# GpSimd's three-part splits and bias additions as two instructions each

## The reference

```
x = layernorm(x + self_attention(x))        # 16 heads of 16, ALiBi bias on the keys
x = layernorm(x + cross_attention(x, ctx))  # ctx: 16 x 120 x 256, padded keys masked by -1e9
x = layernorm(x + moe(x))                   # 8 experts, 256 -> 1024 -> 256, relu, top 2 by softmax

qh, kh, vh = x @ Wq + bq, kv @ Wk + bk, kv @ Wv + bv
scores     = qh . kh / 4 + bias;   attn = softmax(scores);   out = (attn @ vh) @ Wo + bo
```

## Time and profile before

| | |
|---|---|
| median of 3 runs | 1312.58 us (1311.31 to 1317.23) |
| the profiled execution's own time | 1317.72 us |
| its span, first to last instruction | 1315.8 us |
| busy in the span: PE, DVE | 1088.9 us (83%), 976.3 us (74%) |
| busy in the span: ACT, POOL | 567.6 us (43%), 489.3 us (37%) |
| granted TensorE clock over the span | 0.933 of full speed |

### The profile page before, as it was taken

One profiled execution on the slowest core, in us unless ns is written; L12 is line 12 of the kernel. 1 busy time (PEld: TensorE's weight loads), 2 busy tenths in 40 slices (PEclk: granted clock), 3 DMA queues, 4 the chain that ended last, 5 costly groups with the idle time before them and its releaser, 6 DMA issues. The chain is left out here.

```text
span 1315.8 us, 32466 instructions
## 1 busy us (share of the span) xinstructions
PE 1088.9 (83%) x9894; PEld 773.2 (59%) x9895; DVE 976.3 (74%) x2213; ACT 567.6 (43%) x1025; POOL 489.3 (37%) x603
## 2 busy tenths in 40 slices
PE   3778989999888889989998661889999999999970
PEld 2445666666665566656665441667777777777750
DVE  1568888888887888888887663577777777777754
ACT  1434555555554566666665420223222323232325
POOL 1233343334433435545552574022322322322224
PEclk7889999999999899999998865899999999999995
DMA  8577866686648488879886676652222222222228
GB/s 179 136 179 162 193 141 180 175 206 135 164 96 188 114 234 240 196 218 262 240 207 196 205 244 234 247 166 45 40 44 43 43 43 42 42 44 40 45 30 259
DMA packets 153666, 193.98 MB, mean 147 GB/s; under 512 B 30636, under 2 KB 133948, under 8 KB 149323
## 3 DMA queue, kind: packets, MB, share of 16 engines
q1 hardware_dynamic: 139144, 174.67, 49.8%
q0 software_dynamic: 13296, 17.83, 8.1%
q10 hardware_dynamic: 1152, 0.53, 0.2%
HBM read 122.63 MB, written 66.16 MB: 143 GB/s over the span
## 5 line engine op out<-in xcount | busy, mean ns | idle before, releaser
L1397 PE MATMUL HB<-xhi,W 128*128 128x128 f16 x2272 | 292.0, 221 | 21.6 <-issue 16.6
L1397 PEld LDWEIGHTS HB<-xhi,W 128*128 x2272 | 202.0, 98 | 66.1 <-issue 48.1
L1602 POOL DMA_INDIRECT d_sums<-ysc,tok x71 | 111.0, 1563 | 322.3 <-ACT ysc L1463 208.5
L1397 PE MATMUL HB<-xlo,W 128*128 128x128 f16 x1136 | 225.0, 220 | 0.0
L836 DVE TENSOR_REDUCE peaks<-SA 128x4 f32<-128x1024 f32 x128 | 156.6, 1223 | 65.9 <-PE SA L688 65.4
L1113 ACT ACTIVATE PT<-SB 128x1024 f32<-128x1024 f32 x128 | 131.1, 1024 | 130.9 <-PE SB L736 128.9
L1397 PEld LDWEIGHTS HB<-xlo,W 128*128 x1136 | 111.9, 98 | 49.7
L1519 DVE SCALAR_TENSOR_TENSOR hlo<-HB,hhi 128x512 f16<-128x512 f32 x142 | 98.2, 692 | 55.4 <-ACT hhi L1455 51.6
L1455 ACT ACTIVATE hhi<-HB 128x512 f16<-128x512 f32 x142 | 84.2, 593 | 119.7 <-DVE HB L1511 119.5
L1463 ACT ACTIVATE ysc<-yb,wv 128x256 f32<-128x256 f32 x71 | 36.1, 508 | 192.0 <-DVE yb L1543 183.9
L1511 DVE SCALAR_TENSOR_TENSOR HB<-HB,SC,b1c 128x512 f32<-128x512 f32 x142 | 107.1, 754 | 13.9 <-PE HB L1397 7.9
(11 more groups left out here) (205 smaller groups left out, 2375.0 us busy)
## 6 DMA issues: line engine op xcount, KB each, us to landing
wst<-in_w SPq DMA_DIRECT2D x32, 1024.0 KB, 10.1
d_w<-w SPq DMA_DIRECT2D x16, 1024.0 KB, 8.2
W<-d_w SPq DMA_DIRECT2D x16, 1024.0 KB, 7.2
k_stack<-d_k SPq DMA_DIRECT2D x96, 128.0 KB
XB<-d_rows SPq DMA_DIRECT2D x65, 130.0 KB
d_q<-q_part SPq DMA_DIRECT2D x16, 384.0 KB, 6.0
d_k<-k_part SPq DMA_DIRECT2D x16, 384.0 KB, 2.7
q_stack<-d_q SPq DMA_DIRECT2D x16, 384.0 KB, 4.5
```

Of the source, the lines that this page charges most:

```text
L1397: mm = pe.matmul(out, w.rearrange("p e n -> p (e n)"), x[n % 2][:, k, :], start=(k == 0 and half == 0 and x is xhi), stop=(k == KT - 1 and ...
L1602: pool.indirect_dma_start(YS, bass.IndirectOffsetOnAxis(ap=tok[n % 6][:, 0:1], axis=0), ysc[n % 2][:, :], None, compute_op=ALU.add).then_i ...
```

## The change

A split is done in six instructions rather than three, each of the three operations once for feature half 0 and once for half 1. The wait between operations comes behind both halves, so the two halves of one operation stand back to back, with no wait between. `x1bo` and `xbo` are done in two instructions each, one for each of the two token tiles (QT = 2); the semaphore rises with the second. The arithmetic, the tensors and the DMAs are the same. 221 GpSimd instructions are added (63 x 3 + 32).

```
--- before.py
+++ after.py
@@ -1185,11 +1185,16 @@
             if not on(b):
                 return
             wait(pool, f"part0_{n}", b + 1)
-            chain(pool.tensor_tensor(rest[n][:, :, :], full[n][:, :, :], part[n][:, :, 0, :], ALU.subtract))
-            chain(pool.tensor_tensor(part[n][:, :, 1, :], rest[n][:, :, :],
-                                     minus[:, 2:3].unsqueeze(1).to_broadcast([P, KT, width[n]]), ALU.add))
-            pool.tensor_tensor(part[n][:, :, 2, :], rest[n][:, :, :], part[n][:, :, 1, :], ALU.subtract
-                               ).then_inc(sem(f"parts_{n}"), 1)
+            for k in range(KT):
+                chain.put(pool.tensor_tensor(rest[n][:, k, :], full[n][:, k, :], part[n][:, k, 0, :], ALU.subtract))
+            chain.wait()
+            for k in range(KT):
+                chain.put(pool.tensor_tensor(part[n][:, k, 1, :], rest[n][:, k, :],
+                                             minus[:, 2:3].to_broadcast([P, width[n]]), ALU.add))
+            chain.wait()
+            for k in range(KT):
+                ins = pool.tensor_tensor(part[n][:, k, 2, :], rest[n][:, k, :], part[n][:, k, 1, :], ALU.subtract)
+            ins.then_inc(sem(f"parts_{n}"), 1)
 
         def deviations(c, b):
 
@@ -1217,18 +1222,18 @@
             if on(i - 1):
                 wait(pool, "x1", i)
                 wait(pool, "read_Oc", i - 1)
-                pool.tensor_tensor(x1bo[:, :, :], x1s[:, :, :],
-                                   rows_b[:, 3, :].unsqueeze(1).to_broadcast([P, QT, D]), ALU.add
-                                   ).then_inc(sem("x1bo"), 1)
+                for t in range(QT):
+                    ins = pool.tensor_tensor(x1bo[:, t, :], x1s[:, t, :], rows_b[:, 3, :], ALU.add)
+                ins.then_inc(sem("x1bo"), 1)
             split("ck", i)
             if on(i):
                 if isinstance(i, int) and i == 0:
                     pool.wait_ge(sem("ld_rows"), 64)
                 wait(pool, "ld_x", 16 * (i + 1))
                 wait(pool, "read_O", i)
-                pool.tensor_tensor(xbo[:, :, :], xrow[:, :, :],
-                                   rows_b[:, 1, :].unsqueeze(1).to_broadcast([P, QT, D]), ALU.add
-                                   ).then_inc(sem("xbo"), 1)
+                for t in range(QT):
+                    ins = pool.tensor_tensor(xbo[:, t, :], xrow[:, t, :], rows_b[:, 1, :], ALU.add)
+                ins.then_inc(sem("xbo"), 1)
             if i == 2:
                 route_constants()
             if 10 <= i < B:
```

## The result

The changed kernel takes 1322.5 us in the median of 10 runs (1319.9 to 1325.2), the kernel before 1311.6 us in 10 runs (1305.5 to 1317.2). The ratio is 1.0069, 95% interval 1.0050 to 1.0088: slower by 9 us. A second timing of both kernels gave 1.0071 (1.0050 to 1.0093). Ratios leave out the executions that ran over 1.5% above the fastest of their kernel, one of bias_only (1346.2 us) and one of the kernel before (5713.3 us). The forecast, 1314.6 us with a range of 1306 to 1324, holds the time, but its likeliest case, "within 0.5%", did not come: the slower side did, to which I had given 0.20. The profiled execution took 1325.2 us, its span is 1323.4 us and the granted clock 0.927.

What follows compares the result with a forecast made beforehand. TensorE was taken to set the pace, with VectorE close behind. Terms of +1.8, +1.7, +0.2 and -1.6 made +2.1, say +2 us on the 1312.6 us median: 1314.6 us, own range 1308 to 1320, widened to 1306 to 1324.

Steps and rivals of the forecast that it cites:

- within 0.5%: Whole kernel: the change stays within 6.6 us of no change either way; chance 0.70.
- the second rival: VectorE is refused across both back-to-back GpSimd halves, so no stall shortens: some +10 us, 1322; chance 0.07.
- Size of the halves: GpSimd's halves take 0.67, 0.61 and 0.73 us, each pair 0.15 us longer than one instruction; GpSimd 33 us busier.
- The later stacks: Each split's stack reaches TensorE 0.45 us later, counting only at the start and two exposed cq_stack waits: +1.8 us.
- cover: In most steps TensorE's wait for copy L861, right behind the cq_stack wait, absorbs the stack's 0.45 us.
- The copy beside the cq split: VectorE's copy L861 ends 0.30 us later in nine steps, 0.25 earlier in four: +1.7 us.
- The copy beside the k split: VectorE's copy slips through by 0.04 us (-0.12), loses 0.45 in three steps, gains 0.17 in four: +0.2 us.
- Stalls elsewhere: VectorE: L887's stall beside `x1bo` goes, worth 0; copy at 450.90 -0.8, two more places -0.4 each: -1.6 us.
- misses everywhere: All VectorE copies beside cq and k splits miss the gap, and TensorE's clock falls: +15.4 us, 1328; chance 0.13.
- GpSimd keeps hold over both halves: Back-to-back halves never free what VectorE is refused; a pair acts like one longer instruction: some +10 us, 1322; chance 0.07.
- The stalls count in full: VectorE's stalls limit the attention part; L887's 1.10 us in eleven steps gives -12 us, 1301; chance 0.10.
- Nothing reaches the path: The halves' fixed part overlaps and the copies stay as they are: 0 us, 1312.6, inside the forecast's own range.

Runs made afterwards that it cites:

- bias_only: The kernel before with only the two bias additions `x1bo` and `xbo` halved, splits whole: 1330.3 us, ratio 0.9948 (0.9923 to 0.9972).
- cq_later: The kernel before, splits whole, with one small addition inside each cq split so its stack comes 0.46 us later: 1340.0 us, ratio 1.0021 (0.9986 to 1.0056).
- early_only: The kernel before with only the splits of blocks 0 and 1 halved: 1319.3 us, ratio 1.0037 (1.0010 to 1.0063).
- cq_only: The kernel before with only the cq splits halved: 1338.6 us, ratio 1.0012 (0.9981 to 1.0043).
- after_again: The changed kernel, unedited, timed and profiled again: 1323.6 us, ratio 1.0071 (1.0050 to 1.0093) to the kernel before.
- shift_cq_k: The changed kernel with a very short instruction ahead of each cq and k split: 1320.1 us, ratio 1.0050 (1.0027 to 1.0073) to the kernel before.
- halves_at_8: The kernel before with q and cq splits halved and cq ahead of q, in step 8 alone: 1312.0 us, ratio 0.9975 (0.9952 to 0.9997).
- halves_at_8_bias: The kernel before with step 8's q and cq splits halved, cq first, plus `x1bo` and `xbo` halved in every step: 1308.8 us, ratio 0.9961 (0.9940 to 0.9983).
- before_again: The kernel before, unedited, profiled again on the same chip as others of its group: 1307.4 us in its one run.

## Why the prediction was right or wrong

The time is in the range, the sum is not the cause: it gave +2 us where the change costs 9. The measured 1322.5 us lies above the forecast's own 1308 to 1320 and is held by the widening up to the second rival, whose 1322 it meets and whose mechanism the traces refute. That part is luck. Point by point, in the order of the sum:

- *Size of the halves*: right. Forecast 0.67, 0.61 and 0.73 us; the means are 0.672, 0.612 (0.70 in the q split and 0.66 in the cq split, where VectorE holds it up) and 0.734. Pairs take 1.30, 1.18 and 1.41. GpSimd's 37 us against 33 is the ck split (0.485 for a halved addition) and the halves that VectorE delays.
- *The later stacks*, +1.8: **this is the term that failed**. Its cover in the steady steps held: 0.06 us a step in cq_later. Two of its places were mis-sized. The start was +0.45 and is about +5 (early_only 1.3 to 8.3): I counted one stack's lateness, where seven halved splits count, and no clock. Step 8 was +0.9 and is +2.8 by the table, and 6.1 when it is undone by the order, which then also keeps the faster chain's gain: I had counted the lateness, and missed that VectorE's faster chain brings TensorE to the same wait sooner, and that the clock falls behind these 4 us of waiting.
- *The copy beside the cq split*, +1.7: right, in each part. +0.28 in the early steps (forecast +0.30), -0.25 in the late ones, cq_only 0.28 a step.
- *The copy beside the k split*, +0.2: right by the copy (+0.43 in three steps where +0.45 was forecast, -0.12 where it slipped), and silent on what may follow: two falls of the clock in after_again, 1.5 us each, of which it is not shown that the longer waits brought them. shift_cq_k prices the two copy terms together at 3.5 us, of which 0.6 in steps 3 to 8 is what it gains over the kernel before; the sum has 1.9.
- *Stalls elsewhere*, -1.6: half right. The copy at 450.90 gave 0.3 us, not 0.8, since it still waits for a half of `x1bo` (0.97 us in the changed kernel). The copy of the first step (0.59 to 0.45 us) and that of the last (0.61 to 0.53) gave 0.2 and 0.1 us of wait, not 0.4 each. As forecast TensorE did not profit from the end of the stall of the earlier trace rows. Missing from the list was the largest such place, VectorE's chain in step 8, 2 to 2.6 us at L688.

With the measured sizes the sum comes near: start +4.9, the copies with their clock +3.5, step 8 +2.8, biases -1.8 (halves_at_8 against halves_at_8_bias, inside its error) give +9.4, against +9.0 by the first ratio and +9.3 by the second. Each of the timed terms has an error of 2 to 3.5 us, so that it comes this near is partly chance.

Of the rivals, *misses everywhere* had the right sign and perhaps part of the mechanism, lower clock at longer waits. But the copies missed only where the forecast had them miss, and the two falls of after_again came without more misses. *GpSimd keeps hold over both halves* is dead: the late copy of 0.42 us and the subtraction of 0.73, which ends after the first half of `x1bo`, pass between two halves. The rule that I weighed there (the Trainium skill, GPSIMD Engine Reference, section 2.1, Instruction dispatch) speaks of when a Q7 core starts its next instruction; no trace here shows that VectorE is kept out across that start. *The stalls count in full* is dead as a sum (VectorE 24 us less busy, the kernel 9 us slower) and true at one place, step 8. *Nothing reaches the path* is refuted.

## What to carry to other kernels

Before a stage that TensorE waits for is made longer, by however little, look at the granted clock behind its waits, in more than one execution: here a fall of the clock cost 1.5 us a time in the steady part, in one of two profiles of the changed kernel, and the halved splits at the start cost some 5 us, about half of it clock by my estimate. Cutting an instruction that keeps another engine out helps only at the place where that engine is the bound; find that place (here one step of nineteen), cut there alone, and look at which wait is late next, since the time won at one wait is given back at the next stack unless its producer moves ahead in its queue as well. A gain from splitting may also depend on a few hundredths of a microsecond between the second half's start and the other engine's request, and one tiny instruction ahead can move it.

## What the runs showed of the hardware

While a GpSimd addition or subtraction over SBUF runs, VectorE's bf16 copy (0.42 us alone, up to 1.27), its small float32 subtraction (0.17 alone, 1.27) and its scalings of 128x3 float32 and int32 (L964 and L966, 0.39 and 0.53 us beside halves, 0.94 and 1.08 beside whole instructions) stand still until it ends; the copy then ends 0.28 us behind it. Not all do: L970 took 0.21 us at 389.31 in before_again, inside a GpSimd instruction from 389.20 to 390.35. Between two GpSimd instructions back to back the hold (which of the two may run) changes hands, if VectorE asks before the second has taken hold: `x1bo`'s first half took 0.73 us and the subtraction that had asked 0.01 us after its start took 0.73 too. The Trainium skill says (SBUF — State Buffer, section Who interferes with whom) that the port pair shared by the two is an exclusive lock and the only source of contention between them; the trace agrees as far as the lock goes (1.27 us for the subtraction beside a whole `x1bo`, 0.73 beside halves), and adds this hand-over. It works in both directions: a pair of additions alone takes 1.18 us (263.67), one with a copy between its halves 1.40 (538.15).

One program's executions differ at the start by more than half of this change: the two profiles of before stand 5.9 us apart at the product of step 3, with 41 and 31 us at the lower clock ahead of it. And one chip ran every version some 22 us slower (1335.8 against 1313), 3 to 7 us of it between steps 10 and 15 and most of the rest behind them; why is open.
